# 32-head attention in a four-layer kernel: spare rows of the stacks come by transfer, rotated halves go straight to the stacks

## The reference, cut to what matters

```
def _L2_xattn_ref(x, ctx, pos_map, ctx_pos_map, Wq, Wkv, Wout, bout):
    q = (x @ Wq).reshape(b, n, 32, 8)
    k, v = jnp.split(ctx @ Wkv, 2, axis=-1)      # k, v: (b, 256, 32, 8)
    q = apply_axial_rope(q, pos_map)             # pairs turned by an angle from the position
    k = apply_axial_rope(k, ctx_pos_map)
    logits = jnp.einsum('bqhd,bkhd->bhqk', q, k) / sqrt(8)
    attn = jnp.einsum('bhqk,bkhd->bqhd', jax.nn.softmax(logits, -1), v)
    return attn.reshape(b, n, 256) @ Wout + bout
```

## Time and profile before

| | |
|---|---|
| median of 3 runs | 1075.69 us (1073.72 to 1078.15) |
| profiled execution | 1076.64 us, its span 1074.5 us |
| busy: TensorE / VectorE / GpSimd / ScalarE | 830.0 / 710.2 / 431.1 / 377.6 us |
| chain that ended last, by engine | TensorE 41%, issue 21%, VectorE 17%, GpSimd 9%, transfers 5%, ScalarE 5% |
| main memory read / written | 67.74 MB / 19.45 MB, 81 GB/s over the span |

### The profile page before, as it was taken

One profiled execution on the slowest core, in us unless ns is written; L12 is line 12 of the kernel. 1 busy time (PEld: TensorE's weight loads), 2 busy tenths in 40 slices (PEclk: granted clock), 3 DMA queues, 4 the chain that ended last, 5 costly groups with the idle time before them and its releaser, 6 DMA issues.

```text
span 1074.5 us, 12916 instructions
## 1 busy us (share of the span) xinstructions
PE 830.0 (77%) x4202; PEld 521.2 (49%) x4202; DVE 710.2 (66%) x1130; ACT 377.6 (35%) x822; POOL 431.1 (40%) x297
## 2 busy tenths in 40 slices
PE   5786888741988888885698447899875875979993
PEld 2232333331767667664586314454433664645661
DVE  5998999788988888888565833567845554422222
ACT  1523322240444434443454202466540530213331
POOL 4006666101566666664198501333520231152331
PEclk8987888855999999998699775899997996789997
DMA  5103224380122221220100242314126001043114
GB/s 200 44 1 117 78 79 146 166 299 0 43 76 79 79 73 46 77 78 0 69 1 4 64 87 34 128 35 130 35 65 221 2 8 52 6 158 102 45 45 146
DMA packets 28674, 83.77 MB, mean 78 GB/s; under 512 B 3376, under 2 KB 17216, under 8 KB 27104
## 3 DMA queue, kind: packets, MB, share of 16 engines
q1 hardware_dynamic: 26224, 75.35, 21.8%
q0 software_dynamic: 2256, 6.18, 1.6%
q10 hardware_dynamic: 144, 1.57, 0.4%
HBM read 67.74 MB, written 19.45 MB: 81 GB/s over the span
## 4 chain that ended last, share of the span: by engine, by line
PE 41%; issue 21%; DVE 17%; POOL 9%; DMA 5%; ACT 5%; SPq 1%; DVEq 0%; POOLq 0%; ACTq 0%
PE ps L1682 6%; PE ps L512 6%; POOL M L675 4%; PE ps L1328 4%; PE ps L391 3%; PE ps L505 3%; PE ps L895 3%; PE ps L783 2%; DVE Z L314 2%; POOL ZT L978 2%; PE ps L1347 2%; DVE M L644 2%; ACT N L1753 1%; PE ps L1724 1%; DVE M L652 1%
## 5 line engine op out<-in xcount | busy, mean ns | idle before, releaser
L783 PE MATMUL ps<-W,F 128*128 128x256 f32 x544 | 150.8, 402 | 53.6 <-POOL F L738 30.7
L783 PEld LDWEIGHTS ps<-W,F 128*128 128x128 f32 x544 | 101.6, 197 | 86.6 <-DVE W L851 42.3
L586 POOL TENSOR_TENSOR M<-M 128x1024 f32<-128x1024 f32 x32 | 75.3, 2355 | 94.4 <-DVE M L466 53.6
L682 POOL TENSOR_TENSOR W<-W,M 128x1024 f32<-128x1024 f32 x32 | 75.4, 2356 | 84.5 <-DVE M L652 84.5
L1753 ACT ACTIVATE N<-ps 128x512 f32<-128x512 f32 x128 | 69.5, 594 | 107.1 <-PE ps L1686 107.1
L1682 PE MATMUL ps<-M,W 32*128 32x256 f32 x512 | 78.8, 440 | 36.3 <-DMA W<-rot_scratch 17.4
L1774 DVE TENSOR_REDUCE W<-ps 128x4 f32<-128x1024 f32 x64 | 78.1, 1221 | 24.0 <-PE ps L1682 16.8
L644 DVE TENSOR_TENSOR_SCAN M<-ps,M 128x512 f32<-128x512 f32 x64 | 78.0, 1219 | 21.4 <-POOL M L675 21.4
L815 ACT ACTIVATE F<-ps 128x128 f32<-128x128 f32 x136 | 37.8, 278 | 149.7 <-PE ps L783 149.7
L770 PE MATMUL ps<-W,F 128*128 128x256 f32 x272 | 83.2, 389 | 0.0
L1682 PEld LDWEIGHTS ps<-M,W 32*128 32x128 f32 x512 | 49.6, 205 | 67.2 <-issue 39.2
(11 more groups left out here) (272 smaller groups left out, 1779.3 us busy)
## 6 DMA issues: line engine op xcount, KB each, us to landing
M<-dbl_scratch SPq DMA_DIRECT2D x48, 512.0 KB, 3.8
W<-in_gu SPq DMA_DIRECT2D x1, 4800.0 KB, 16.8
W<-in_gu SPq DMA_DIRECT2D x1, 4352.0 KB, 13.7
att_scratch<-W SPq DMA_DIRECT2D x32, 128.0 KB
slot_scratch<-in_slots SPq DMA_DIRECT2D x1, 3999.0 KB, 19.2
M<-slot_scratch SPq DMA_DIRECT2D x3, 1032.0 KB, 9.3
W<-in_gu SPq DMA_DIRECT2D x2, 1536.0 KB, 6.7
W<-in_dn SPq DMA_DIRECT2D x1, 2176.0 KB, 18.4
```

Source lines behind the costliest of these rows:

```text
L586: nc.gpsimd.tensor_tensor(dBu[:, t, :], du[0][:, t, :], Bb[:, par, :], ALU.mult).then_inc(S("dBu_rdy"), 1)
L682: nc.gpsimd.tensor_tensor(u[1][:, t, :], u[1][:, t, :], hC[:, t, :], ALU.add).then_inc(S("y1_acc"), 1)
L783: last = nc.tensor.matmul(up, ztt[:, par, c, :], gu[:, c, s, :], start=(c == 0), stop=(c == DC - 1))
```

## The change

The scratch tensors in main memory and the two fills of GpSimd are gone. A new constant input `spare` with two rows of 8192 numbers (ones, zeros) is laid out on the host, and SP writes the spare rows from it in eight transfers of 24 partitions x 8192 numbers (four for `kst`, then four for `qst`), ahead of the halves. The first 8 partitions of a batch are not written by them. The halves go in four transfers each from `rot` to the stack, within the chip's memory. VectorE's wait before it writes a `rot` buffer again is now for the four transfers of `stack0` or `stack1`, and TensorE waits for `spare_rows` as well.

```
@@ rotate @@
             if x >= 2:
-                dve.wait_ge(S(f"rot_out{c}"), 16)
+                dve.wait_ge(S(f"stack{c}"), 16 * BATCH)
@@ attn2_stacks_sync @@
             sp.dma_start(dn, a["dn2"]).then_inc(S("ld_f2_down"), 16)
+            for stack, value in ((kst, 0), (qst, 1)):
+                for b in range(BATCH):
+                    row = a["spare"][value:value + 1, :].to_broadcast([32 - HD, HEADS * SEQ])
+                    sp.dma_start(stack[32 * b + HD:32 * b + 32].rearrange("p h n -> p (h n)"), row).then_inc(S("spare_rows"), 16)
             for x in range(4):
                 c, stack = x % 2, (kst, qst)[x // 2]
                 sp.wait_ge(S("rot_rdy"), x + 1)
-                sp.dma_start(rot_dram[x], rot[:, c, :]).then_inc(S(f"rot_out{c}"), 16)
-                sp.wait_ge(S(f"rot_out{c}"), 16 * (x // 2 + 1))
-                if x in (0, 2):
-                    sp.wait_ge(S("keys_ones") if x == 0 else S("queries_clear"), 1)
-                src = rot_dram[x].rearrange("(d h) (b n) -> b d h n", d=HD, b=BATCH)
                 for b in range(BATCH):
-                    sp.dma_start(stack[32 * b:32 * b + HD, 16 * c:16 * (c + 1), :], src[b]).then_inc(S(f"stack{x}"), 16)
+                    sp.dma_start(stack[32 * b:32 * b + HD, 16 * c:16 * (c + 1), :],
+                                 rot[:, c, b * SEQ:(b + 1) * SEQ]).then_inc(S(f"stack{x}"), 16)
@@ attn2_gpsimd @@
-            nc.gpsimd.memset(kst, 1.0).then_inc(S("keys_ones"), 1)
-            nc.gpsimd.memset(qst, 0.0).then_inc(S("queries_clear"), 1)
@@ attn2_tensor @@
             pe.wait_ge(S("v_rdy"), 4)
-            pe.wait_ge(S("stack0"), 4 * 16)
-            pe.wait_ge(S("stack2"), 4 * 16)
+            pe.wait_ge(S("stack0"), 16 * BATCH)
+            pe.wait_ge(S("spare_rows"), 2 * 16 * BATCH)
+            pe.wait_ge(S("stack2"), 16 * BATCH)
@@ lay_out @@
+    a["spare"] = np.repeat(np.array([[1.0], [0.0]], f32), HEADS * SEQ, axis=1)
```

More of the change, by code:

```diff
@@ L234, in flamingo @@
         assert m.at <= HEADS * TOK // 2
-        rot_dram = [nc.dram_tensor(f"rot_scratch{x}", (P, TOK), F32, kind="Internal").ap() for x in range(4)]
         attU = M[:, 0:2 * TOK].rearrange("p (c n) -> p c n", c=DC)
@@ L1731, in attn2_tensor @@
                 if h == 16:
-                    pe.wait_ge(S("stack1"), 4 * 16)
-                    pe.wait_ge(S("stack3"), 4 * 16)
+                    pe.wait_ge(S("stack1"), 16 * BATCH)
+                    pe.wait_ge(S("stack3"), 16 * BATCH)
                 if h < HEADS + 2:
```

## The result

The changed kernel took 1086.34 us (median of 4 runs, 1083.62 to 1092.77) against 1075.01 us for the kernel before; the ratio is 1.0114, 95% interval 1.0084 to 1.0143: slower, by 12 us. The forecast was 1089, 12.7 us over before. The profiled execution (1092.77 us, span 1090.9) is the slowest of the four; 2.75 us of its excess stand ahead of the stage in question, since `dn2` is issued at 592.30 in place of 589.55. I therefore measure the stage from the issue of `dn2` to the first matmul of the scores, and call that the **lead**. Before it is 647.80 - 589.55 = 58.3 us; after it is 665.27 - 592.30 = 73.0. From the first scores to the end of the span there are 426.7 us before and 425.6 after, so behind the scores nothing got slower: in these two profiles the lead grew by 14.7 us, while the medians differ by 11.3.

A forecast was written before the change was run, and what follows sets the result against it. The chain to the first scores was taken as the bound, shifting the end one for one. Constants (40 us) and three halves (8.7 each) put scores at 660.5, 12.7 later: 1076.64 + 12.7, said as 1089; range 1084 to 1095, 8-in-10 1072 to 1101.

The forecast's parts named there:

- Fills gone: Normalised tiles on VectorE: without GpSimd's fills the first takes about 0.4 us, not 12.0; work behind can come 11.6 us earlier.
- The spare rows: Eight 768 KB transfers queued ahead of the halves: 8 x 5.0 = 40 us, ending at 633.5.
- the Trainium skill's rule: Spare-row transfers: neighbouring partitions share a port of 27.2 GB/s, so the eight take 38.5 us, scores 1.5 us sooner.
- Halves: Copies from `rot` to the stacks within chip memory: 8.7 us for each half, as the destination seems to set it.
- The waits in a row: VectorE's last two rotations wait for `stack0` (643.1) and `stack1` (651.8); the scores wait for `stack2` (660.5).
- Sum: Start of the scores at 660.5, 12.7 us later than 647.8, passed on whole to the end: 1089 us.
- A: Rival: spare rows at the engines' rate, 24 us instead of 40; scores 3.3 us sooner, 1073.3; chance 0.10.
- B: Rival: spare rows slow, but a half takes 4.0 us from chip memory; start +0.7 us, 1077.4; chance 0.12.
- C: Rival: spare rows and halves both fast; scores 15 us sooner, 1061; chance 0.05.
- D: Rival: copies within the chip take 13 us, 1102, or spare rows go at 86 GB/s, 1122; chance 0.13.

The follow-up runs named there:

- e5: Kernel before, with GpSimd's two fills started only after VectorE has written the eight normalised tiles; ratio to before 0.9970.
- e3: Changed kernel, with the constants written in two transfers over all 128 partitions, each ahead of the first half of its stack; ratio to before 0.9939.
- e6: Kernel before, with GpSimd's fills after the normalised tiles and the halves sent straight from chip memory, no constants transferred; ratio to before 0.9902.
- e7: Kernel before, with the halves sent straight from chip memory and both fills done by ScalarE; ratio to before 0.9868.
- e9: As e7, with each transfer's 8 rows written 4 partitions apart, so scores come from misplaced rows; ratio to before 0.9769.
- e4: Changed kernel, with constants and halves of batches 2 and 3 issued on ScalarE's queue beside SP's; ratio to before 1.0063.
- e12: Changed kernel, with constants in two transfers over 128 partitions and the halves' rows in steps of 4 partitions; ratio to before 0.9791.
- e1: Kernel before, with only the halves sent straight from chip memory and GpSimd's fills kept; ratio to before 0.9931.
- e8: As e7, with the halves of batches 2 and 3 issued on ScalarE's queue; ratio to before 0.9836.

## Why the prediction was right

*Fills gone.* The tiles ended 10.4 us behind the issue of `dn2` (11.0 forecast), and TensorE was through with the queries at 621.9, 29.6 us behind it (29.1 forecast):

```profile
665.27 2.11 PE L1680 MATMUL ps<-M,W 32*128 32x256 f32 x16 [43.33 <-DMA W<-W]
```

e5 shows that the fills made the wait, which in the prediction was only argued from the two ends at 609.3 and 609.2. Its gain was indeed covered by the transfers.

*The spare rows.* 40 us were forecast from the one transfer of `dn3b`, 40.1 follow from the windows. e3 shows that the set of partitions decides, which the prediction had as the reading of a row with several possible causes. The estimate of 38.5 us by the Trainium skill's rule ("SBUF — State Buffer", section on the DMA port swizzle) was a little low. The eight issues took SP 3.8 us (592.67 to 596.44) where 2.6 were taken, without effect.

*Halves.* Forecast 8.7 us each; `stack0`, `stack1` and `stack2` were seen at 647.45, 656.44 and 665.14, so 9.0 and 8.7 apart. Main memory or chip memory as the source makes little difference: just under 9 us for a half before, 8.7 to 9.7 directly in the changed kernel, e6 and e7. That the destination sets it is shown by e9.

*The waits in a row.* Forecast 53.6, 62.3 and 71.0 us behind `dn2`; measured 55.2, 64.1 and 72.8. Of the 1.9 us, 1.6 come ahead of `stack0`, and they are what is left of two misses that partly cancel. The constants ended 42.5 us behind the issue of `dn2` (634.8 - 592.3), 1.5 us sooner than the 44.0 forecast, so the later landing of `dn2` (5.8 us behind its issue in place of 4.4) did not hold them back. But from the end of the constants to the sight of `stack0` there are 12.7 us where 9.6 were forecast. 1.8 of these 3.1 us are the gap from 634.8 to 636.6, for which the prediction had no term; it let the half flow at once behind the constants. In e4 there is such a gap too, from 634.4 to 635.8 without data. What makes it, and where the other 1.3 us go, is open.

*Sum.* Lead +14.7 where +12.7 was forecast; time +12 by the ratio, against +12.7. The nearness of the last two is partly luck, since the profiled lead alone would say +14.7. The first scores, forecast for 658 to 663, came at 665.27, or at 662.5 without the 2.75 us ahead of `dn2`. The range of 1084 to 1095 is not worked out at its lower end: the rule it names gives 1.5 us less than 1089, and the rest of the 5 us has no term. Rivals A, B, C and D are out for the change as written: A needed over 200 GB/s, B and C a half in under 6 us, D a half in 13 us or constants at 86 GB/s. e3, e9 and e12 show that B's and C's leads were within reach, but only with another set of partitions.

## What to carry to other kernels

Ask which partitions a transfer writes before counting its bytes: here 24 partitions at a time took twice as long for three quarters of the bytes of 128, and 8 partitions in steps of 4 were two and a half times as fast as 8 neighbours. Before moving a fill from an idle engine to the transfer queue, ask what is queued behind it; here three short transfers, and through a buffer's wait the rotations too, stood behind 40 us of constants. When an instruction takes many times its usual duration, look for the engine whose work ends at the same moment, and try moving that work before replacing it.

## What the runs showed of the hardware that was not expected

- VectorE's tile waited through both fills of GpSimd, not only the one under way: it began at 597.3, the first fill ended at 602.3, the tile at 609.3. The rotation's last step, which began at 596.2 during the first fill, took its usual 1.23 us.
- A fill of 128 x 8192 numbers takes ScalarE 7.03 us (e7), as good as GpSimd's 6.93, and leaves VectorE alone.
- With constants queued on the transfer engines, SP stood too: one issue of a 128 KB transfer took 17.02 us in the changed kernel and at most 1.67 in e3, against 0.77 in e1, where no constants are queued.
- The same halves on one queue were 8.7 to 9.7 us apart from kernel to kernel (after, e6, e7); why is open.
- Two queues gave the constants 3% (162 against 157 GB/s). Halves with pieces of 1 KB went at up to 110 GB/s on two queues in e4, behind constants, but at 55 to 65 in e8, with nothing ahead of them; the difference is open.
